# Spreading the degree factors of a graph layer through a line in memory, and collecting its adjacency from a high and a low part

## The reference

```python
A = adj + jnp.eye(n)
deg = jnp.sum(A, axis=-1)
deg_safe = jnp.where(deg == 0, 1.0, deg)
dinv = jnp.where(deg == 0, 0.0, deg_safe ** (-0.5))
norm_adj = dinv[:, :, None] * A * dinv[:, None, :]
support = jnp.einsum('bnd,de->bne', x, W)
out = relu(jnp.einsum('bnm,bme->bne', norm_adj, support) + b)
```

## Time and profile before

| | us |
|---|---|
| median of 3 runs | 357.98 |
| lowest and highest run | 357.45 and 364.82 |
| the profiled execution | 358.44 |
| its span | 356.6 |
| its mean granted TensorE clock | 0.988 of full |

### The profile page before, as it was taken

The page is one execution under the profiler, slowest core; times in us unless marked ns, Lnnn a source line. Parts: engine busy times, 40 slices in busy tenths (PEclk is TensorE's granted clock), DMA queues, the critical chain, the costliest instruction groups (busy, mean ns, idle before and its releaser), DMA issues. The chain is left out here.

```text
span 356.6 us, 6244 instructions
## 1 busy us (share of the span) xinstructions
PE 339.5 (95%) x1767; PEld 275.7 (77%) x1767; DVE 319.4 (90%) x566; ACT 236.8 (66%) x410; POOL 94.2 (26%) x153
## 2 busy tenths in 40 slices
PE   4989999999999999999999999999999999999891
PEld 1577678986889688977988688968897798866670
DVE  2989999999999999999999899999999999896636
ACT  4383665748856696748764885669684886976752
POOL 4750001604050503222050505040231306052123
PEclk9989999999999999999999999999999999999997
DMA  6914241514043222604161403412260415301101
GB/s 195 307 26 130 83 132 44 170 31 148 18 129 129 74 76 61 211 0 147 36 202 34 147 13 103 156 55 92 55 193 25 147 31 147 119 22 36 29 2 53
DMA packets 30950, 33.95 MB, mean 95 GB/s; under 512 B 4884, under 2 KB 18124, under 8 KB 30932
## 3 DMA queue, kind: packets, MB, share of 16 engines
q1 hardware_dynamic: 30166, 33.55, 31.3%
q10 hardware_dynamic: 766, 0.18, 0.2%
HBM read 24.85 MB, written 4.40 MB: 82 GB/s over the span
## 5 line engine op out<-in xcount | busy, mean ns | idle before, releaser
L1276 POOL TENSOR_TENSOR base<-mv,vscale 128x4 f32<-128x4 f32 x16 | 6.0, 373 | 234.9 <-DVE mv L1405 228.2
L685 PE MATMUL p_outer<-t_h,w_h 128*128 128x344 f32 x131 | 41.9, 337 | 0.0
L685 PE MATMUL p_outer<-t_h,w_l 128*128 128x344 f32 x131 | 40.8, 328 | 0.0
L1373 DVE TENSOR_TENSOR am<-am,adj 128x512 f32<-128x512 f32 x64 | 40.0, 686 | 0.0
L1539 DVE TENSOR_TENSOR am_l<-am,am_h 128x2048 fp32r<-128x2048 f32 x15 | 34.3, 2287 | 1.8 <-ACT am_h L1130 1.8
L685 PE MATMUL p_middle<-t_h,w_h 128*128 128x344 f32 x90 | 28.6, 329 | 0.0
L1130 ACT ACTIVATE am_h<-am 128x2048 fp32r<-128x2048 f32 x15 | 28.5, 1901 | 0.0
L685 PE MATMUL p_middle<-t_h,w_l 128*128 128x344 f32 x90 | 28.0, 322 | 0.0
L685 PEld LDWEIGHTS p_outer<-t_h,w_h 128*128 128x128 f32 x131 | 25.0, 194 | 2.4 <-ACT t_h L1002 0.7
L1108 ACT ACTIVATE yoo<-yn,nb,rs 128x128 f32<-128x128 f32 x63 | 25.8, 483 | 0.0
L685 PEld LDWEIGHTS p_outer<-t_h,w_l 128*128 128x128 f32 x131 | 25.2, 195 | 0.3
(11 more groups left out here) (387 smaller groups left out, 1019.4 us busy)
## 6 DMA issues: line engine op xcount, KB each, us to landing
adj<-adjT SPq DMA_DIRECT2D x64, 256.0 KB, 3.2
xpad<-xT SPq DMA_DIRECT2D x17, 256.0 KB, 2.9
out<-yoo SPq DMA_DIRECT2D x16, 256.0 KB, 2.3
crossed<-left SPq DMA_DIRECT2D x31, 48.0 KB
left<-left SPq DMA_DIRECT2D x30, 48.0 KB
right<-left SPq DMA_DIRECT2D x30, 48.0 KB
wc<-w_c SPq DMA_DIRECT2D x2, 384.0 KB, 6.6
wraw<-g_w SPq DMA_DIRECT2D x1, 640.0 KB
```

The source lines that it names most:

```text
L685: return nc.tensor.matmul(out_, w, x, start=start, stop=stop, skip_group_check=True)
L1276: TT(base[:, 0:CH], mv[:, :, 1], vscale[:, 0:CH], ALU.mult)
L1373: TT(am[:, c, :], am[:, c, :], adj[:, c, :], ALU.mult).then_inc(s_am[c], 1)
```

## The change

The diagonal matrices and the spread product go. SP writes dinv, transposed, into a new line [8, 106] in memory, waits for it, and reads it back to all 106 rows, into the tile where diag stood (now `factors`). DVE multiplies ac by it in step 14, ahead of the masks. ACT and DVE then split ac into a high and a low part, into the tiles t_h and t_l, whose last use is in step 14; SELT goes, rounded to fp32r, into val_h. The combine is four fp32r products and stands behind the gh product.

```diff
-        diag = part(he[:], 0, CC, CC)
+        factors = part(he[:], 0, CC, CC)
+        ac_h, ac_l, selt_h = part(t_h[:], 0, CC, CC), part(t_l[:], 0, CC, CC), val_h[0:CC, 0:64]
+        line = nc.dram_tensor("line", (PAIRS, CC), fp32).ap()
...
         class GroupsPE:
-            def spread(self, pe, mm):
-                pe.wait_ge(s_diag, 2)
-                for h in range(2):
-                    mm(BC_BANKS[h][0:CC, 0:HP * CC], cst[0:CC, C_SAME:C_SAME + CC], diag[:, pairs(h), :]).then_inc(s_spread, 1)
             def combine(self, pe, mm):
                 for h in range(2):
-                    pe.wait_ge(s_columns, h + 1)
-                    mm(MSEL_BANKS[h][0:64, 0:HP * CC], cst[0:CC, C_SELT:C_SELT + 64], ac[0:CC, pairs(h), :]).then_inc(s_combined, 1)
+                    pe.wait_ge(s_diag, h + 2); pe.wait_ge(s_ac, h + 2)
+                    to = MSEL_BANKS[h][0:64, 0:HP * CC]
+                    mm(to, selt_h, ac_h[:, pairs(h), :], True, False)
+                    mm(to, selt_h, ac_l[:, pairs(h), :], False, True).then_inc(s_combined, 1)
...
         class GroupsAct:
             def degree_factors(self, act):
-                act.wait_ge(s_dinv, 2); act.wait_ge(s_t3h, PAIRS); act.wait_ge(s_t3l, PAIRS)
-                for j in range(PAIRS):
-                    last = nc.scalar.activation(diag[:, j, :], cst[0:CC, C_ID:C_ID + CC], ACT.Identity, scale=dinv[:, j:j + 1])
-                last.then_inc(s_diag, 1)
+                act.wait_ge(s_left, PAIRS)
+                nc.scalar.activation(selt_h, cst[0:CC, C_SELT:C_SELT + 64], ACT.Copy)
+                act.wait_ge(s_dinv, 2)
                 for j in range(PAIRS):
                     last = nc.scalar.activation(ac[0:CC, j, :], ac[0:CC, j, :], ACT.Identity, scale=dinv[:, j:j + 1])
                 last.then_inc(s_diag, 1)
+            def columns_high(self, act):
+                act.wait_ge(s_sum[0], PAIRS); act.wait_ge(s_sum[4], PAIRS); act.wait_ge(s_sum[3], PAIRS)
+                for h in range(2):
+                    act.wait_ge(s_columns, h + 1)
+                    nc.scalar.activation(ac_h[:, pairs(h), :], ac[0:CC, pairs(h), :], ACT.Copy).then_inc(s_diag, 1)
...
         class GroupsDVE:
             def columns(self, dve):
+                dve.wait_ge(s_diag, 1); dve.wait_ge(s_spread, 32)
                 for h in range(2):
-                    dve.wait_ge(s_spread, h + 1)
-                    nc.vector.tensor_tensor(ac[0:CC, pairs(h), :], ac[0:CC, pairs(h), :], banked(BC_BANKS[h], CC, CC), ALU.mult).then_inc(s_columns, 1)
+                    nc.vector.tensor_tensor(ac[0:CC, pairs(h), :], ac[0:CC, pairs(h), :], factors[:, pairs(h), :], ALU.mult).then_inc(s_columns, 1)
+            def columns_low(self, dve):
+                dve.wait_ge(s_sum[0], PAIRS); dve.wait_ge(s_sum[4], PAIRS); dve.wait_ge(s_sum[3], PAIRS)
+                for h in range(2):
+                    dve.wait_ge(s_columns, h + 1); dve.wait_ge(s_diag, h + 2)
+                    nc.vector.tensor_tensor(ac_l[:, pairs(h), :], ac[0:CC, pairs(h), :], full(ac_h[:, pairs(h), :]), ALU.subtract).then_inc(s_ac, 1)
...
         SP, at the start of a step
+                if static(b, B - 2):
+                    sp.wait_ge(s_dinv, 2)
+                    sp.dma_start(line.rearrange("j c -> c j"), dinv[:], allow_slow_non_contiguous=True).then_inc(s_spread, 16)
+                    sp.wait_ge(s_spread, 16); sp.wait_ge(s_t3h, PAIRS); sp.wait_ge(s_t3l, PAIRS)
+                    sp.dma_start(factors, line.unsqueeze(0).broadcast_to([CC, PAIRS, CC])).then_inc(s_spread, 16)
...
         PE, step 15
-                    g_pe.spread(pe, mm)
...
                 gate(p_gi, "n", 0, cb_h, cb_l, True, False)
-                if static(b, B - 1):
-                    g_pe.combine(pe, mm)
                 after(pe, s_ghb, n(0)); gate(p_gh, "n", 2, xb_h, xb_l, True, True).then_inc(s_gx, 1)
+                if static(b, B - 1):
+                    g_pe.combine(pe, mm)
                 turn(n)
...
         ACT, end of an even step
                 gates(n)
+                if static(b, B - 2):
+                    g_act.columns_high(act)
...
         DVE, even step
                 conv_low(n)
+                if static(b, B - 2):
+                    g_dve.columns(dve)
                 for c in range(CH):
                     mask(n, 1, c)
...
         DVE, odd step
                 keep_share(v, n, -1)
+                if not more:
+                    g_dve.columns_low(dve)
                 result(n, -1)
-                if not more:
-                    g_dve.columns(dve)
                 mask_low(n)
```

More of the change, by code:

```diff
@@ L262, in gnn_kernel @@
         s_gmv = sem("s_gmv"); s_gbase = sem("s_gbase"); s_grs = sem("s_grs"); s_gst = sem("s_gst")
-        BC_BANKS = MSEL_BANKS = (p_outer, p_middle)
+        MSEL_BANKS = (p_outer, p_middle)
         TR_BANKS = (p_outer, p_middle, p_z)
```

## The result

The changed kernel takes 369.36 us in the median of 4 runs (366.06 to 370.36), the kernel before 357.82; the ratio is 1.0302, with a 95% interval of 1.0258 to 1.0346. It is slower by 11.5 us in the medians. The forecast was 363.6 with a range of 357 to 373: inside the range, in the right direction, but with half of the loss missing. Two things in it came out less well than the range says. 369.36 lies above the forecast's own range (360.8 to 368.5), and only the wide one, which takes in rival 3 and part of rival 2, holds it. And "slower by over two per cent", which came, had been given 0.40, "within two per cent" 0.58.

What follows compares the result with a forecast made beforehand. The DVE, ACT and POOL chain to the tail's first tanh was taken as the bound, not TensorE. Masks 6.75 us later, less 1.0 regained, added 5.7 to 358.44: 364.1, or 363.6 for the median; range 357.0 to 373.

Steps and rivals of the forecast that it cites:

- the forecast's own range: Whole kernel, both transfers on two engines and packet cost within the profile's rows: 360.8 to 368.5 us, chance 0.55.
- rival 3: Last batch: idle TensorE loses its clock, matmuls up to the tail about 5 us late, 368.5 us; chance 0.09.
- rival 2: First transfer: tiny writes cost 52 ns each, 22 us in all, +21.8 us, 379.8 us; chance 0.13.
- above 365.1: Whole kernel slower by over two per cent: some 0.2 of the forecast's 0.55, plus rival 2 and rival 3; chance 0.40.
- delta = F - 315.1: Shift of the tail's first tanh, F being the second transfer's landing, 320.8: +5.7 us; break-even at 315.1.
- the slack I found: Last batch, ahead of the tail: TensorE done with its part 1.7 us before ACT asks for it.
- Rival 1: Step 14: both transfers spread over 16 engines, landing at 309.1, no stall, -0.6 us, 357.4 us; chance 0.19.
- Rival 4: Whole kernel: no stall, TensorE the bound to the end, -2.2 us and 0.5 of its wait, 355.3 us; chance 0.04.

Runs made afterwards that it cites:

- the two halves of the 112-row experiment: Changed kernel with only the first transfer on 112 rows: 363.84 us; with only the second transfer on 112 rows: 358.15 us.

## Why the prediction was half right

**The place and the cause of the loss were right.** The profile after shows the steps one by one: n_h of batch 14 moved 0.47 us nearer to the adjacency issues (0.55 forecast), yn without a wait, the masks behind the second transfer, a share of 0.13 for it (0.12), and a landing at 322.7 (320.8). One sign came otherwise: the share of 0.12 was foretold for all of 305 to 320, and it stands only from 317 on; the first transfer shows 0.20 to 0.27 and then 0.00 from 308 to 312. Two engines for 106 rows, read from a 25-row store and a trickle early in the kernel, is borne out by the copy's share and by the two halves of the 112-row experiment. A slip in the chances changes nothing: the parts named for "above 365.1" (0.2, 0.13 and 0.09) add up to 0.42, not 0.40.

**The terms of the stall.** The first transfer's packets began at 303.3, 1.3 us before the 304.6 forecast, and took 4.7 us (to 308.0), where 5.9 were forecast from 14 ns a packet: 11 ns. Its landing was put at 0.4 us and took 3.6: the term that was wrong by most, taken from a store of full rows. The copy took 11.1 for 9.9. The rate of two engines was right: its 106 packets of 3.4 KB run from 314.7 to 322.2, 7.5 us for 7.4, and what is too much lies ahead of the first of them. Together the copy landed 1.9 us later than forecast, two errors partly cancelling two others. DVE stood ready at 314.2, 0.35 earlier than forecast, and the stall was 8.56 us for 6.2.

**The slack ahead of the tail.** delta = F - 315.1 gave 7.6 us for the measured F; 7.3 came. The masks moved 8.68 and the tanh 7.31, so the time regained between them is 1.4 us, not 1.0. The run in which TensorE was kept busy is the forecast's own world, a stall with a full clock, and took 364.0 us against 363.6. That is no luck of the stall alone: with its copy landing at 321.3 the same sum gives 364.1.

**The step that failed.** The prediction said of the idle TensorE: "3.4 us at half speed lose 1.7 us of work, just the slack I found, so my sum has nothing for it". For the last batch the conclusion held, though the clock stayed low for longer, from 322.4 to 332.6, 4.9 us of it under matmuls: TensorE's last product for the first tanh ends at 338.17, ACT's share ahead of that tanh at 338.18, so the slack was used up to the last and nothing more. What the step left out is that the clock would fall a second time. It did, from 346 to 356 us, where the tail's products are the chain and no slack covers them, after it had been back at 1.00 for 13.7 us. That is the missing 4.5 us. Rival 3 had the mechanism and nearly the price, but put it in the last batch and gave it 0.09. Its sign, a clock near 0.5 for more than 4 us there, was met, and yet cost nothing there. The working of its 5 us isn't shown, either (7.9 us of matmuls at half speed, less the 1.7 of slack, would be 6.2). That its 368.5 lies near the 369.4 measured is luck.

**The rivals.** Rival 1 (wide transfers, 357.4) is what happens with 112 rows: 358.0. Its landing did not come as it said, 12.4 us behind the first issue and not 7.5; the time is right because 12.4 was still 0.6 us early enough. Rival 2 had the right suspicion, that tiny writes are dearer than any row, but the dearness is in the landing, not in the time per packet. Rival 4 (TensorE is the bound) falls: 1.4 us of products put back cost nothing. Its 2.2 us exist, but they lie idle behind POOL's powers, as the prediction had it, and come to light in part only when the share moves.

**What stays open.** Why the clock falls again in the tail. Filling the idle time prevents it in all four runs (363.2 to 365.1 us), so the idle time is its condition, but it isn't certain to follow: the version with only the first transfer widened ran at 0.50 in the last batch and had 1.00 in the profile's tail. Three of its four runs lie at 363.3 to 364.3 and one at 367.65, whose mean clock was lower (0.970 against 0.985). Likewise the changed kernel's fastest run, 366.06, has a mean clock of 0.982 against 0.961 to 0.966 in the others.

## What to carry to other kernels

A transfer through memory that stands in for a matmul must be costed as a chain of two landings, with the number of rows asked first: here the copy to 106 rows held a share of 0.12, two of 16 engines, and took 11.1 us, and the copy to 112 rows took 5.3. Ask also what is written: single elements of 4 bytes landed 2.6 to 4.3 us behind their last packet. Count also what stands behind a slow transfer in the same queue, and whether an idle TensorE will run its next chain at full clock. And before time on a 95% busy engine is saved, follow what the next stage's first instruction waits for: here it was POOL, through a small instruction ahead of it on ACT.

## What the runs showed that was not expected

- Elements of 4 bytes written to memory: 848 of them were seen 10.6 us behind their issue (9.2 and 9.5 in two other profiles, the last 2.6 and 2.7 of them silent), 896 over sixteen engines still 7.3 to 7.7, but the same values as 106 rows of 32 B on two engines in 3.2 us. In the first case nothing moved in the last 3.6 us of the wait. The Trainium skill (DMA: Bandwidth & Descriptors, Specifications) puts its boundary at 512 B, below which the DMA reads, modifies and writes; both forms lie far below it, and the runs show a difference of over 4 us between them. Whether the DMA did so here, no run shows.
- A slow transfer holds up what stands behind it in the same queue: in step 1 a 256 KB load landed after 10.4 us instead of 2.9 and came 7.9 us too late. In step 14 of the changed kernel the load of W1 behind the copy took 12.7 us instead of 4.4; no engine waited for it.
- TensorE ran dry at 319.5, had its clock at 1.2 GHz from 322.4 to about 332.6, was back at 2.4 GHz, and fell to 1.2 again at 346 for ten microseconds, though it had been busy for 64 to 100% of every microsecond from 340 to 346.
